# A stacked pair multiply whose first pair is taken block by block while the weights are combined

## What is computed

```python
y = x + einsum('bct,bcd->bdt', x, cond_weights[cond[b]])
out = y + einsum('btd,od->bto', y, W) + scal[a] * ((y @ A[a].T) @ Bm[a].T)
```

## Time and profile before

| | |
|---|---|
| median of three runs | 821.88 us |
| the profiled execution | 821.71 us, span 819.8 us |
| TensorE busy with matmuls | 776.4 us, 95% |
| VectorE, ScalarE, GpSimd busy | 66%, 47%, 19% |
| granted TensorE clock, mean | 0.989 |
| HBM read and written | 58.72 MB, 33.55 MB |

### The profile page before, as it was taken

How to read it: one execution, slowest core, us unless ns; L and a number is a source line. 1 busy time by engine, 2 the same in 40 slices (tenths; PEclk the granted TensorE clock), 3 DMA queues, 4 the chain that set the end, 5 groups by cost and what they waited for, 6 DMA issues and landing times.

```text
span 819.8 us, 16303 instructions
## 1 busy us (share of the span) xinstructions
PE 776.4 (95%) x5216; PEld 714.1 (87%) x5216; DVE 537.9 (66%) x921; ACT 383.0 (47%) x712; POOL 152.8 (19%) x297
## 2 busy tenths in 40 slices
PE   0489999999999999999999999999999999999996
PEld 0479999999999999999999999999999999999995
DVE  4965667666666766666677666666666667666663
ACT  3634454544444444444454544545444454544442
POOL 4620122221012222102222201222220122221000
PEclk9889999999999999999999999999999999999999
DMA  7043323333322333332233333233333223333211
GB/s 288 0 136 110 102 86 116 134 134 116 120 83 99 118 134 131 106 130 79 101 125 134 128 109 114 76 114 131 134 128 109 97 89 115 134 134 113 67 59 78
DMA packets 43748, 92.50 MB, mean 113 GB/s; under 512 B 7380, under 2 KB 23764, under 8 KB 43220
## 3 DMA queue, kind: packets, MB, share of 16 engines
q1 hardware_dynamic: 43588, 92.30, 32.5%
q10 hardware_dynamic: 144, 0.00, 0.0%
HBM read 58.72 MB, written 33.55 MB: 113 GB/s over the span
## 4 chain that ended last, share of the span: by engine, by line
PE 93%; DVE 3%; DMA 2%; SPq 1%; issue 0%; ACT 0%; DVEq 0%
PE beta L625 35%; PE delta L641 22%; PE beta L638 11%; PE alpha L625 11%; PE o_ps L669 4%; PE o_ps L667 4%; PE o_ps L668 4%; PE delta L649 2%; DMA w_raw<-wB 1%; DVE w_raw L567 1%; PE alpha L652 1%; PE beta L652 1%; DVE wn_lo L574 1%; DVE wr_lo L570 1%; PE xaT_ps L679 0%; DMA out<-o_sb 0%
## 5 line engine op out<-in xcount | busy, mean ns | idle before, releaser
L310 POOL TENSOR_TENSOR wr_lo<-a_ride,wr_hi 128x192 fp32r<-128x192 f32 x32 | 21.2, 664 | 608.2 <-ACT wr_hi L352 608.2
L625 PE MATMUL beta<-wr_hi,s_hi 128*128 128x256 f32 (+1 forms) x512 | 105.7, 288 | 13.1 <-DVE xa_part L484 12.4
L625 PE MATMUL beta<-wr_lo,s_hi 128*128 128x256 f32 (+1 forms) x512 | 105.1, 287 | 0.0
L625 PE MATMUL beta<-wr_hi,s_lo 128*128 128x256 f32 (+1 forms) x512 | 105.1, 286 | 0.0
L641 PE MATMUL delta<-wn_hi,s_hi 128*128 128x512 f32 x256 | 103.1, 403 | 0.0
L641 PE MATMUL delta<-wn_hi,s_lo 128*128 128x512 f32 x256 | 100.4, 392 | 0.0
L641 PE MATMUL delta<-wn_lo,s_hi 128*128 128x512 f32 x256 | 100.1, 391 | 0.0
L558 DVE COPY o_sb<-o_ps 128x512 f32<-128x512 f32 x64 | 43.8, 684 | 83.1 <-PE o_ps L669 80.3
L625 PEld LDWEIGHTS beta<-wr_hi,s_hi 128*128 128x128 f32 x512 | 83.3, 191 | 16.1 <-issue 12.6
L625 PEld LDWEIGHTS beta<-wr_lo,s_hi 128*128 128x128 f32 x512 | 81.4, 191 | 0.0
L625 PEld LDWEIGHTS beta<-wr_hi,s_lo 128*128 128x128 f32 x512 | 80.9, 190 | 0.0
(11 more groups left out here) (118 smaller groups left out, 1885.8 us busy)
## 6 DMA issues: line engine op xcount, KB each, us to landing
out<-o_sb SPq DMA_DIRECT2D x64, 512.0 KB, 2.7
x_even<-xT SPq DMA_DIRECT2D x32, 512.0 KB, 4.0
x_odd<-xT SPq DMA_DIRECT2D x32, 512.0 KB, 4.0
b_raw<-lora_b SPq DMA_DIRECT2D x192, 64.0 KB, 2.1
w_raw<-wB SPq DMA_DIRECT2D x4, 1024.0 KB, 8.8
a_now<-lora_a SPq DMA_DIRECT2D x64, 64.0 KB, 2.3
c_raw<-cond_w SPq DMA_DIRECT2D x64, 64.0 KB, 1.9
s_tab<-scalings ACTq DMA_DIRECT2D x1, 4.0 KB, 2.8
```

Of the source, the lines that this page charges most:

```text
L310: nc.gpsimd.tensor_tensor(ride_of(wr_lo, J1, J2), a_ride[:, :, 0:3, :], ride_of(wr_hi, J1, J2), ALU.subtract).then_inc(ride_ready, 1)
L625: last = nc.tensor.matmul(bank[:, h, 0:hi - lo], left[:, chunk + k, :], right[:, k, lo:hi], start=opens and k == 0 and left is left_hi and ...
```

## The change

Pair 0 no longer goes through `step`. It is multiplied plainly, by eight block products, in an opening on every engine: first with B11 (both samples), then B12, B21, B22, each block as soon as it has landed and is split. TensorE runs `first_left` (256 columns, banks `alpha`, `beta`) and `first_right` (512 columns, banks `delta`, `o_ps[1]`), a LoRA product for each bank, and `times_c` (three matmuls) four times, the fourth between J2 and J1 of pair 1. B11 comes in four loads of 256 KB, the other blocks in two of 512 KB each, x of pair 0 in four of 256 KB. B22 (`w_d`) lies in `x_odd`, and pair 1 uses `x_even`; all slots swap. Adapter rows of pair 0 are loaded from ScalarE's queue.

The weight sums T1 to T4 are made during the opening and in the step of pair 1: T1, T2, T4 on VectorE in two pieces each, T3 on GpSimd in four pieces of 512 columns. B12, B21 and B22 themselves are split too and later overwritten by sums' parts. In all, eight blocks are split where there were seven (2048 columns each). B22's identity is added on GpSimd, behind the adapter columns of pair 1. Pair 0's outputs are stored from `v_sb`, `d1_sb`, `q1_sb` in four stores of 256 KB. Two more pair steps are written out, and the loop has 13 iterations. The steps from pair 2 on are as before.

The diff, cut to its core (indentation taken off; the lines of `step` that now have `if first:` stand for pair 1):

```diff
+        w_a, w_b, w_c = (w_raw[:, n, :, :] for n in range(3))
+        w_d = x_odd[:, :, :, :].rearrange("p n k c -> p (n k c)").rearrange("p (k h) -> p k h", h=H)
...
-sp.dma_start(adapter_sb[:, :], adapter_idx).then_inc(adapter_landed, 16)
-sp.dma_start(w_raw[:, B11, :, :], wB[B11, :, :, :]).then_inc(w_landed[B11], 16)
-load_x(0, 0, 0)
-sp.dma_start(w_raw[:, B21, :, :], wB[B21, :, :, :]).then_inc(w_landed[B21], 16)
+def load_first_x(n, half):
+    k = half * KH
+    sp.dma_start(x_even[:, n, k:k + KH, :], xT[n, :, k:k + KH, :]).then_inc(first_x_landed[2 * half + n], 16)
+def load_w(to, b, pieces):
+    per = KH // pieces
+    for k in range(pieces):
+        sp.dma_start(to[:, k * per:(k + 1) * per, :], wB[b, :, k * per:(k + 1) * per, :])\
+          .then_inc(w_landed[b][k], 16)
+def store_first(n, h, place, count):
+    sp.wait_ge(first_out, count)
+    sp.dma_start(out[n, :, h * H:(h + 1) * H], place).then_inc(first_stored, 16)
-load_a(0, 0, 0)
-sp.dma_start(w_raw[:, B12, :, :], wB[B12, :, :, :]).then_inc(w_landed[B12], 16)
-sp.dma_start(w_raw[:, B22, :, :], wB[B22, :, :, :]).then_inc(w_landed[B22], 16)
-sp.wait_ge(w_lo_ready, 7)
+load_first_x(0, 0)
+sp.dma_start(w_a[:, 0, :], wB[B11, :, 0, :]).then_inc(w_landed[B11][0], 16)
+load_first_x(1, 0)
+for k in range(1, KH):
+    sp.dma_start(w_a[:, k, :], wB[B11, :, k, :]).then_inc(w_landed[B11][k], 16)
+load_w(w_c, B12, 2)
+load_first_x(0, 1)
+load_w(w_b, B21, 2)
+load_first_x(1, 1)
+load_w(w_d, B22, 2)
+sp.dma_start(cond_sb[:, :], cond_idx).then_inc(cond_landed, 16)
 sp.wait_ge(adapter_landed, 16)
 load_b(0, 0, 0)
 load_a(0, 0, 1)
 sp.wait_ge(cond_landed, 16)
+load_c(0, 0, 0)
+sp.wait_ge(first_x_ready, 4)
 load_x(0, 0, 1)
+load_b(0, 0, 1)
+load_c(0, 0, 1)
+store_first(0, 0, v_sb[:, :], 1)
+store_first(1, 0, flat(d1_sb[:, :, :]), 2)
+store_first(0, 1, flat(q1_sb[:, :, :]), 3)
+store_first(1, 1, v_sb[:, :], 4)
+sp.wait_ge(t2_summed, 2)
+sp.wait_ge(t3_summed, KH)
+load_x(0, 0, 2)
+load_a(0, 0, 2)
...
+scale_ride(0, 0, 0, ((3, 0, 0), (4, 1, 0), (0, 0, KH), (1, 1, KH)))
+pool.wait_ge(ride_hi_ready, 1)
+rest_last_ride()
+pool.wait_ge(ride_hi_ready, 2)
+beside = slice(J1 * RS + H, J1 * RS + H + 2 * R)
+nc.gpsimd.tensor_tensor(wr_lo[:, :, beside], a_ride[:, :, 0:2, :].rearrange("p k s r -> p k (s r)"),
+                        wr_hi[:, :, beside], ALU.subtract).then_inc(ride_ready, 1)
+subtract_ride(0, 0, 0)
 nc.gpsimd.memset(b_raw[:, :], 0.0).then_inc(zeros_ready, 1)
 nc.gpsimd.memset(xa_cols[:, :], 0.0).then_inc(zeros_ready, 1)
+pool.wait_ge(ride_ready, 2)
+scale_ride(0, 0, 1, usual)
+subtract_ride(0, 0, 1)
+for k in range(2):
+    pool.wait_ge(w_landed[B22][k], 16)
+diagonal = bass.AP(x_odd, 0, [[KH * H, P], [H + P, KH], [1, P]])
+nc.gpsimd.tensor_tensor(diagonal, diagonal, ident[:, :].unsqueeze(1).to_broadcast([P, KH, P]),
+                        ALU.add).then_inc(b22_added, 1)
+pool.wait_ge(b22_added, 1)
+pool.wait_ge(w_lo_ready, M12)
+pool.wait_ge(t1_summed, 2)
+sum_t3(0)
+rest_ride(0, 0, 1)
+for k in range(1, KH):
+    sum_t3(k)
...
+            evacuate_first(v_sb[:, :], o_ps[1][:, :], 4)
+            hi_of_t3()
...
+act.dma_start(adapter_sb[:, :], adapter_idx).then_inc(adapter_landed, 16)
 act.dma_start(s_tab[:, :], scalings.to_broadcast([P, NAD])).then_inc(s_landed, 16)
+act.wait_ge(adapter_landed, 16)
+for n in range(2):
+    adapter = act.value_load(adapter_sb[0:1, n:n + 1], min_val=0, max_val=NAD - 1)
+    act.dma_start(a_now[:, n, :, :], lora_a[bass.ds(adapter, 1), :, :, :].rearrange("a p k r -> (a p) k r"))\
+       .then_inc(a_landed, 16)
+hi_of_first_x(x1_hi[:, 0:KH, :], 0, 0)
+for k in range(KH):
+    act.wait_ge(b11_added, k + 1)
+    nc.scalar.activation(wr_hi[:, k, J2 * RS:J2 * RS + H], w_a[:, k, :], ACT.Copy).then_inc(w_hi_ready, 1)
+    if k == 0:
+        hi_of_first_x(s1_hi[:, :, :], 1, 0)
+act.wait_ge(a_scaled, 2)
+nc.scalar.activation(wr_hi[:, :, J2 * RS + H:RW],
+                     a_ride[:, :, 3:5, :].rearrange("p k s r -> p k (s r)"), ACT.Copy)\
+    .then_inc(ride_hi_ready, 1)
+act.wait_ge(a_scaled, 4)
+nc.scalar.activation(wr_hi[:, :, J1 * RS + H:J1 * RS + H + 2 * R],
+                     a_ride[:, :, 0:2, :].rearrange("p k s r -> p k (s r)"), ACT.Copy)\
+    .then_inc(ride_hi_ready, 1)
+for half in range(2):
+    act.wait_ge(w_landed[B12][half], 16)
+    hi_of(wr_hi[:, :, J6 * RS:J6 * RS + H], w_c, half)
+hi_of_first_x(x1_hi[:, KH:KC, :], 0, 1)
+for half in range(2):
+    act.wait_ge(w_landed[B21][half], 16)
+    hi_of(wr_hi[:, :, J1 * RS:J1 * RS + H], w_b, half)
+hi_of_first_x(a22_hi[:, :, :], 1, 1)
+act.wait_ge(b22_added, 1)
+for half in range(2):
+    hi_of(wn_hi[:, J5, :, :], w_d, half)
+act.wait_ge(b_landed, 96)
+nc.scalar.activation(b_stack[:, :], b_raw[:, :], ACT.Copy).then_inc(b_hi_ready, 1)
+for half in range(2):
+    act.wait_ge(t1_summed, half + 1)
+    hi_of(wn_hi[:, J3, :, :], w_a, half)
+act.wait_ge(c_summed, 1)
+nc.scalar.activation(c_hi[:, :, :], c_raw[:, :, :], ACT.Copy).then_inc(c_hi_ready, 1)
+ride(0, 0, 1)
+act.wait_ge(mask_ready, 12)
+act.wait_ge(first_xaT, 1)
+nc.scalar.activation(g_first[:, :], xaT_ps[:, 0:P], ACT.Copy, scale=mask[:, 0:1]).then_inc(first_g, 1)
+nc.scalar.activation(g_second[:, :], xaT_ps[:, 0:P], ACT.Copy, scale=mask[:, 1:2]).then_inc(first_g, 1)
+act.wait_ge(first_lora, 1)
+nc.scalar.activation(as_halves(flat(s3_hi[:, :, :])), halves(alpha), ACT.Copy).then_inc(first_z_hi, 1)
+act.wait_ge(first_lora, 2)
+nc.scalar.activation(as_halves(flat(s4_hi[:, :, :])), halves(beta), ACT.Copy).then_inc(first_z_hi, 1)
+split_x1(0, 0, 1)
+nc.scalar.activation(flat(s2_hi[:, :, :]), delta[:, :], ACT.Copy).then_inc(first_z_hi, 1)
+evacuate_first(v_sb[:, :], o_ps[0][:, :], 1)
+act.wait_ge(first_product, 8)
+nc.scalar.activation(flat(s3_hi[:, :, :]), o_ps[1][:, :], ACT.Copy).then_inc(first_z_hi, 1)
+evacuate_first(flat(d1_sb[:, :, :]), xaT_ps[:, :], 2)
+evacuate_first(flat(q1_sb[:, :, :]), alpha[:, 0, :], 3)
+split_s2(0, 0, 1)
+act.wait_ge(first_product, 6)
+for half in range(2):
+    act.wait_ge(t2_summed, half + 1)
+    hi_of(wr_hi[:, :, J4 * RS:J4 * RS + H], w_a, half)
...
+            rest_of(MT3, wr_lo[:, :, J6 * RS:J6 * RS + H], w_c, wr_hi[:, :, J6 * RS:J6 * RS + H])
...
+            for half in range(2):
+                nc.vector.tensor_tensor(two(w_b, half), two(w_b, half), two(w_a, half),
+                                        ALU.subtract).then_inc(t4_summed, 1)
...
+add_identity_b11(0)
+rest_of_first_x(x1_lo[:, 0:KH, :], 0, 0, x1_hi[:, 0:KH, :], 1)
+add_identity_b11(1)
+rest_of_b11(0)
+rest_of_first_x(s1_lo[:, :, :], 1, 0, s1_hi[:, :, :], 2)
+add_identity_b11(2)
+rest_of_b11(1)
+add_identity_b11(3)
+rest_of_b11(2)
+rest_of_b11(3)
+rest_of(M12, wr_lo[:, :, J6 * RS:J6 * RS + H], w_c, wr_hi[:, :, J6 * RS:J6 * RS + H])
+dve.wait_ge(w_lo_ready, M12)
+for half in range(2):
+    nc.vector.tensor_tensor(two(w_a, half), two(w_c, half), two(w_a, half), ALU.subtract)\
+        .then_inc(t1_summed, 1)
+rest_of_first_x(x1_lo[:, KH:KC, :], 0, 1, x1_hi[:, KH:KC, :], 3)
+rest_of(M21, wr_lo[:, :, J1 * RS:J1 * RS + H], w_b, wr_hi[:, :, J1 * RS:J1 * RS + H])
+rest_of_first_x(a22_lo[:, :, :], 1, 1, a22_hi[:, :, :], 4)
+rest_of(M22, wn_lo[:, J5, :, :], w_d, wn_hi[:, J5, :, :])
+dve.wait_ge(zeros_ready, 2)
+dve.wait_ge(first_product, 5)
+split_first_xa(0, alpha[:, 1, Q:Q + R])
+add_identity_c(0, 0)
+rest_b(0, 0)
+dve.wait_ge(first_product, 6)
+split_first_xa(1, beta[:, 1, Q + R:Q + 2 * R])
+rest_of(MT1, wn_lo[:, J3, :, :], w_a, wn_hi[:, J3, :, :])
+rest_c(0, 0)
+rest_of_first_z(1, as_halves(flat(s3_lo[:, :, :])), halves(alpha), as_halves(flat(s3_hi[:, :, :])))
+rest_of_first_z(2, as_halves(flat(s4_lo[:, :, :])), halves(beta), as_halves(flat(s4_hi[:, :, :])))
+rest_x1(0, 0, 1)
+rest_of_first_z(3, flat(s2_lo[:, :, :]), delta[:, :], flat(s2_hi[:, :, :]))
+dve.wait_ge(x_landed[0], 32)
+sum_s1(0, 0, 1)
+sum_s3(0, 0, 1)
+sum_s2(0, 0, 1)
+rest_of_first_z(4, flat(s3_lo[:, :, :]), o_ps[1][:, :], flat(s3_hi[:, :, :]))
+dve.wait_ge(w_lo_ready, MT1)
+for half in range(2):
+    nc.vector.tensor_tensor(two(w_a, half), two(w_d, half), two(w_a, half), ALU.subtract)\
+        .then_inc(t2_summed, 1)
+rest_s2(0, 0, 1)
+rest_of(MT2, wr_lo[:, :, J4 * RS:J4 * RS + H], w_a, wr_hi[:, :, J4 * RS:J4 * RS + H])
...
+            pe.wait_ge(first_out, 3)
+            pe.wait_ge(first_z, 4)
+            times_c(o_ps[1][:, :], 1, flat(s3_hi[:, :, :]), flat(s3_lo[:, :, :])).then_inc(first_o, 1)
...
+pe.wait_ge(first_x_ready, 1)
+for k in range(KH):
+    pe.wait_ge(w_lo_ready, k + 1)
+    first_left(k, 0, alpha, x1_hi, x1_lo, True, J2)
+    if k == 0:
+        pe.wait_ge(first_x_ready, 2)
+    first_left(k, 0, beta, s1_hi, s1_lo, True, J2)
+pe.wait_ge(ride_ready, 1)
+for k in range(KH):
+    last = first_left(k, 1, alpha, x1_hi, x1_lo, True, J2)
+last.then_inc(first_product, 1)
+for k in range(KH):
+    last = first_left(k, 1, beta, s1_hi, s1_lo, True, J2)
+last.then_inc(first_product, 1)
+b12_hi, b12_lo = (w[:, :, J6 * RS:J6 * RS + H] for w in (wr_hi, wr_lo))
```

(71 more changed lines are left out.)

306 lines of the change are left out of this document (177 added, 129 removed).

## The result

The changed kernel takes 803.06 us, the median of four runs (802.51 to 804.07), against 821.81 us (821.57 to 821.96) for the kernel before. The ratio is 0.9774, with a 95% interval of 0.976 to 0.9789. The forecast was 805.5 us in 799.5 to 812.5. The profiled execution is the one at 804.07 us, span 802.3 us.

The account below looks back on a forecast made before the run. The prediction took TensorE's work, 24.07 us a pair, as the bound, leaving pair 2's start to decide. Its steps moved that from 87.3 to 70.9, 16.4 us off 821.7: 805.3, as a median 805.5 us, range 799.5 to 812.5.

Parts of the forecast that it names:

- Step A: TensorE's start: small loads, ScalarE's adapter loads and table load, then first splits; first matmul at 9.0, 13 us sooner.
- Step B: Pair 0's opening on TensorE: 25.8 us of work, 2.5 for low clock, waits; sum 30.3, end at 39.3.
- The cover: B22 split and ready at 28.5, 1.4 us ahead of TensorE's need at about 29.9; its identity added at 26.2.
- Step C: Pair 1's J2, a 0.6 us wait for the fourth `z`, `times_c` and J1, ending at 46.4.
- Step D: New wait before pair 1's J4: VectorE's list delays `xa_part` to 50.9; TensorE stands 4.5 us, clock drops.
- the guess: GpSimd's hold on VectorE before `xa_part`: 0.8 us for each of three late T3 pieces, 2.3 us in all.
- Step E: Pair 1 from J4 at the low clock (5.38 us) through J7 and J5; pair 2 starts at 70.9.
- Slow pieces: Rival: all five MB land at half rate, 5.6 us a MB; B22 lands at 31.2; 811.6 us; chance 0.12.
- The rule of the Trainium skill: Against the smaller loads: batch DMAs to at least 1 MiB; by it the opening would be late as for slow pieces.
- The quick rival: GpSimd holds nobody off and the gap before J4 is too short to drop the clock; 800.7 us; chance 0.22.
- The slow rival: TensorE stays at 1.2 GHz until pair 2, which starts at 97; 831.6 us; chance 0.03.

Follow-up runs that it names:

- the repeat: The changed kernel itself measured once more, unedited, beside other follow-up runs: 803.41 us (802.70 to 804.29).
- the fillers: Eleven unused matmuls of 512 columns added to the changed kernel between J1 and J4 of pair 1: median 802.61 us, ratio 0.9773.
- the three reorderings: Changed kernel with B22's identity ahead of pair 1's adapter columns, xa_part ahead of T3's lo, second adapter columns' split ahead of T4's lo: 804.17 us.
- the four reorderings: As the three reorderings, and in pair 1's step VectorE sums c22 ahead of pair 2's x lo and sums: 800.70 us (799.44 to 800.81).

## Why the prediction was right

*Frame.* The prediction was right to ask for one number, the start of pair 2: forecast 70.9, measured 69.6, and no pair behind it changed its length.

*Step A*, first matmul: forecast 9.0, measured 8.1. ScalarE had its two adapter loads issued by 4.4, not 5.6: the index landed within 1.24 us of its issue, and I had used SyncE's 3.19 as if it were a wait for it. The table load did stand just ahead of the first activation, at 4.40 for 1.28 us. The chain of the changed kernel doesn't pass through it: it goes through the adapter rows. With TensorE kept busy beforehand the first real matmul came a microsecond later, and J4 only 0.4 later; with whole loads it came 1.4 later and J4 no later than in the repeat, though that version's time leaves the point open.

*Step B*, the end of the opening: forecast 39.3, measured 38.5, all of it from step A: the opening took 30.4 us where the sum has 30.3. Its terms met in the middle. Of the 2.0 us of waits the rows show one, 0.6; the slow first matmuls cost about 2.4 as an estimate (from the first matmul to B22's first product 20.4 us, against 18.2 with 0.2 of wait where TensorE had been kept busy), forecast 2.5; the work itself took some 1.6 more than 25.8. The cover, too, was met by two errors of opposite sign. Pair 0's adapter rows took 6.96 us to land behind the weights, not the 2.3 us of the earlier trace rows, which is the median over the whole kernel: they were there 2.7 us late. But from there to the end of the memsets it took 3.4 us, not 8.0, since VectorE stood idle for most of it and GpSimd's four multiplications took 1.05 us. So B22's identity was done at 24.3 in place of 26.2; that the sum of the two came so near is luck. B22 itself landed up to 12.3 us after its issue at 7.3, so near 19.6, not 17.2; nothing noticed, since GpSimd came to it at 23.0. With the identity moved forward it is noticed: it could start only at 18.6.

*Step C*, end of J1: 46.4 against 45.0: 0.8 carried on from step B, and the wait of 0.6 for the fourth `z` part is not there.

*Step D* was the heart: VectorE from B22's `lo` to `xa_part` in 23.6 us, measured 25.40 to 48.97, 23.6 us. The list without GpSimd was 21.3 and measures 21.4. The other 2.3 were the guess for turns with GpSimd; the stretched operations give 2.15. The total was right and its source only in part: the guess put all of it on three T3 pieces, and moving T3 to VectorE shows some 1.5 for them and 0.7 for GpSimd's other operations, which the sum had at nothing. The wait of 4.5 us was 4.1, and the low clock was there; the fillers show that it cost J4 2.5 us.

*Step E*: 20.0 forecast, 20.5 measured (J4 5.64 for 5.38).

*Size.* The gain by medians is 18.75 us, forecast 16.4; 1.3 of the difference is at pair 2, and 1 us is that the profiled execution is the slowest of its four. The 1.3 are 1.9 by which VectorE could begin B22's `lo` sooner (25.4 for 27.3, the cover in step B), less 0.5 in step E; step A's microsecond is not among them.

*Rivals.* Slow pieces: the cost is up to a microsecond of stream, not half the rate, and the version with whole loads was no faster. The rule of the Trainium skill that stood against the smaller loads, to batch them to at least 1 MiB (DMA: Bandwidth & Descriptors, section Bandwidth), points the right way here, 347 to 394 GB/s with pieces and 415 with whole loads, with a small effect. The quick rival's time, 800.7, lies as near to the measured 803.06 as the forecast of 805.5 does (2.4 us each), so the time alone doesn't choose between them. The mechanism does: GpSimd did hold VectorE off, and the clock did fall. The slow rival fell: the slow pace ended at about 13.9, 5.8 us after the first matmul.

*Missed.* The prediction took each wait singly. After J4 the step has a row of further entries in VectorE's list (the transposed columns, c22, z21) that sit close behind the path. They did not show while J4 was late, and they swallowed what `xa_part` moved alone and the three reorderings together had won before J4. It also took the adapter rows for a small load of 2.3 us; they are the start of the chain in the changed kernel, and what it would bring to have them land sooner was not tried.

## What to carry to other kernels

When a late entry in an in-order list is moved forward, follow the list to its next user, and price the operations that now stand ahead of it; here moving `xa_part` alone cost some 2 us, three reorderings together brought nothing and four brought 2.4 us. After each repair read the chain again from its start: moving B22's identity put TensorE's first matmuls on it, and what an experiment had shown to have slack has it no longer. A second engine that shares time with the bound engine is help only by what is left after their turns: measure both engines' operations stretched and alone. Where a short stop of TensorE can't be taken away, filling it with unused matmuls can keep the clock: with the four reorderings in place it brought another 1.3 us, without them no gain over all runs.
